# A swin block on one core: one multiplication of three tiles from VectorE to GpSimd, and one residual ahead of a transposition

## The reference

```python
attn = jax.nn.softmax(scores, axis=-1)
out = jnp.einsum('nhij,nhjd->nhid', attn, v)
out = out.transpose(0, 2, 1, 3).reshape(nw, L, c)
return out @ out_w.T + out_b
...
attn_out = attn_out @ proj_w.T + proj_b
...
y = shortcut + y
```

## Time and profile before

| | us |
|---|---|
| median of 3 runs | 88.78 |
| lowest, highest run | 88.52, 90.08 |
| profiled execution | 87.22 |
| its span, first to last instruction | 85.2 |

### The profile page before, as it was taken

The page is one execution under the profiler, slowest core; times in us unless marked ns, Lnnn a source line. Parts: engine busy times, 40 slices in busy tenths (PEclk is TensorE's granted clock), DMA queues, the critical chain, the costliest instruction groups (busy, mean ns, idle before and its releaser), DMA issues.

```text
span 85.2 us, 4265 instructions
## 1 busy us (share of the span) xinstructions
PE 79.6 (93%) x1786; PEld 48.0 (56%) x1786; DVE 64.7 (76%) x208; ACT 53.0 (62%) x89; POOL 46.8 (55%) x58
## 2 busy tenths in 40 slices
PE   5999999889999999799999999999999999999950
PEld 5987757555865767467566637465464423533420
DVE  4999998969789989989789999997943944333260
ACT  0396798879888476588288356664587664725400
POOL 7988829989862972997634675787204041300000
PEclk9999999999999999999999999999999999999998
DMA  0799600121101122101021120000000000032042
GB/s 19 203 331 439 258 31 8 36 66 33 53 32 53 51 84 78 53 1 38 32 100 56 52 64 6 8 0 8 0 8 0 0 0 0 13 118 86 38 162 84
DMA packets 3490, 5.75 MB, mean 67 GB/s; under 512 B 944, under 2 KB 1712, under 8 KB 3344
## 3 DMA queue, kind: packets, MB, share of 16 engines
q1 hardware_dynamic: 2608, 3.08, 10.9%
q10 hardware_dynamic: 864, 2.40, 7.3%
HBM read 2.66 MB, written 1.05 MB: 44 GB/s over the span
## 4 chain that ended last, share of the span: by engine, by line
PE 65%; DVE 18%; issue 8%; DMA 3%; ACT 2%; SPq 1%; DVEq 0%; ACTq 0%
PE ps_s L333 14%; PE ps_u L426 6%; PE ps_u L499 5%; DVE row_max L656 4%; PE ps_m L307 4%; PE ps_s L483 4%; PE ps_t L333 3%; PE ps_t L483 3%; DMA masked<-qk 3%; PE ps_o L467 3%; PE ps_m L483 2%; PE ps_t L409 2%; PE ps_m L297 2%; PE ps_o L499 2%; PE ps_o L442 2%
## 5 line engine op out<-in xcount | busy, mean ns | idle before, releaser
L1058 POOL TENSOR_TENSOR max_x<-max_t,early 128x512 bf16<-128x512 bf16 x14 | 14.7, 1048 | 10.6 <-DVE max_t L669 10.6
L656 DVE TENSOR_REDUCE row_max<-ps_s 128x16 f32<-128x1024 f32 x15 | 18.1, 1209 | 2.5 <-PE ps_s L333 2.2
L915 ACT ACTIVATE probs<-ps_t 128x1024 f32<-128x1024 f32 x13 | 13.3, 1023 | 8.8 <-PE ps_t L409 8.4
L333 PE MATMUL ps_s<-masked,qk 32*64 32x256 f32 x240 | 16.9, 387 | 1.0 <-ACT probs L915 0.4
L333 PE MATMUL ps_t<-masked,qk 32*64 32x256 f32 x224 | 15.5, 387 | 0.0
L1067 POOL TENSOR_TENSOR rstd<-y_var,minus_half 128x4 f32<-128x4 f32 x8 | 8.1, 1010 | 9.9 <-DVE y_var L719 9.8
L333 PEld LDWEIGHTS ps_s<-masked,qk 32*64 32x64 f32 x240 | 8.1, 131 | 5.9 <-issue 2.9
L426 PE MATMUL ps_u<-probs,vz 128*32 128x64 f32 x512 | 10.5, 222 | 0.0
L426 PEld LDWEIGHTS ps_u<-probs,vz 128*32 128x32 f32 x512 | 7.9, 109 | 3.1 <-issue 2.7
L1043 POOL TENSOR_TENSOR rstd<-var,minus_half 128x4 f32<-128x4 f32 x8 | 8.3, 1043 | 1.0 <-DVE var L644 0.4
L282 PE MATMUL ps_t<-zeros 128*128 128x128 f32 x32 | 6.9, 376 | 1.0 <-DVE zeros L817 1.0
(11 more groups left out here) (111 smaller groups left out, 150.6 us busy)
## 6 DMA issues: line engine op xcount, KB each, us to landing
masked<-qk SPq DMA_DIRECT2D x38, 32.0 KB, 2.0
x_ch<-x_ch_d ACTq DMA_DIRECT2D x1, 1024.0 KB, 8.0
out_d<-result SPq DMA_DIRECT2D x3, 256.0 KB, 2.5
x_tok<-x_tok_d ACTq DMA_DIRECT2D x1, 512.0 KB, 6.0
masked<-qk SPq DMA_DIRECT2D x8, 64.0 KB, 2.4
late<-late_d ACTq DMA_DIRECT2D x1, 352.0 KB, 5.2
x_tok<-x_tok_d SPq DMA_DIRECT2D x2, 128.0 KB, 3.4
x_tok<-x_tok_d ACTq DMA_DIRECT2D x1, 256.0 KB, 4.8
```

The lines of the kernel that those rows point to most:

```text
L333: return nc.tensor.matmul(ps[o:o + L, g, n * TOK:(n + 1) * TOK], qk[r:r + RG, b, w, t], masked[r:r + RG, b, :, w, t], start=(n == 0), stop ...
L656: nc.vector.tensor_reduce(row_max[:, w, 0:16], score_bank(k, w)[:].rearrange("q g (h j) -> q (g h) j", j=L), axis=AX.X, op=ALU.max).then_i ...
L915: nc.scalar.activation(probs[:, w, :], scores_t_bank(k, w)[:].rearrange("q g c -> q (g c)"), ACT.Exp).then_inc(probs_done, 1)
L1058: nc.gpsimd.tensor_tensor(max_x[:, k % 2, w, :].rearrange("q (n i) -> q n i", n=16), bf16_high(max_t[:, w, :]).unsqueeze(1).to_broadcast([ ...
```

## The change

On VectorE `scale_attn(k)` is left out for tiles 3, 4 and 5, and GpSimd does the same multiplication, right behind `spread_max(t+1, 0)` in slots 4, 5 and 6. It waits for the inverted sums of its tile and for `transpose_attn` of the tile before, which read the same buffer `attn_tok`. The semaphore `attn_scaled` is now raised by VectorE for five tiles and by GpSimd for three. Besides, in slot 2 VectorE's `residual(0)` stands ahead of `transpose_sums(1)` instead of behind `split_max(3, 0)`; the residuals of the other tiles stay where they were.

```diff
+        POOL_SCALED = (3, 4, 5)
...
+                if t == 2:
+                    residual(0)
                 if tile_ok(t - 1):
                     transpose_sums(t - 1)
                 if tile_ok(t + 1):
                     split_max(t + 1, 0)
-                if tile_ok(t - 2) and t - 2 not in SPLIT:
+                if t > 2 and t - 2 not in SPLIT:
                     residual(t - 2)
...
-                if tile_ok(t - 1):
+                if tile_ok(t - 1) and t - 1 not in POOL_SCALED:
                     scale_attn(t - 1)
...
+            def scale_attn(k):
+                pool.wait_ge(recip_done, k + 1)
+                pool.wait_ge(attn_done, k)
+                nc.gpsimd.tensor_tensor(attn_tok[:].rearrange("q n (u d) -> q n u d", u=2),
+                                        sums[:, :, 0:2 * D].rearrange("q n (u d) -> q n u d", u=2),
+                                        recip[:].unsqueeze(3).to_broadcast([P, 16, 2, D]),
+                                        op=ALU.mult).then_inc(attn_scaled, 1)
...
                 if tile_ok(t + 1):
                     spread_max(t + 1, 0)
+                if t - 1 in POOL_SCALED:
+                    scale_attn(t - 1)
```

## The result

| | kernel before | changed kernel |
|---|---|---|
| median of 8 runs | 88.87 | 89.17 |
| lowest, highest | 87.69, 90.16 | 88.96, 89.83 |
| span of the profiled execution | 85.2 | 87.7 |

The ratio of the changed kernel to the one before is 1.0233, 95% interval 1.0189 to 1.0278. It compares for each kernel the runs near its fastest, so it says more of the lower ends (88.96 against 87.69, which is 1.4%) than of the medians, which differ by 0.3%. Timed twice more, on two chips, the same changed kernel had ratios of 1.0100 (0.9995 to 1.0205) and 1.0117 (1.0051 to 1.0183); the kernel before, timed against itself, had 1.0066 (1.0015 to 1.0117) and 0.9990 (0.9921 to 1.0058). So by these timings the change costs about 1%, and the comparison itself can be off by more than half a per cent. I had forecast 0.4 us less.

The account below looks back on a forecast made before the run. TensorE, busy 93% of the span, was taken as the bound, with three holes of 0.77 us in all. Gains of 0.26 and 0.14 us summed to 0.40 us, for a forecast of 88.4 us, range 87.7 to 89.3.

Parts of the forecast that it names:

- the other 0.19 us of the hole: TensorE's 0.45 us hole at 34.46: the earlier exponential gains 0.26 us, then the shift of the scores holds the rest.
- part 1: Slot 2, VectorE: tile 0's residual ahead of the transposed sums lets ScalarE's exponential start at 33.48, not 33.74; gain 0.26 us.
- Part 1 brings nothing: Rival: something else holds the exponential in slot 2, leaving 0.14 us gained alone, 88.6 us; chance 0.10.
- Part 2's price: Slots 4 to 6: one GpSimd scaling of tiles 3 to 5 costs 0.61 us, range 0.42 to 1.05; gain 0.14 us.
- starts at about 46.86: Slot 4, VectorE: split_max starts then instead of 47.06, so transpose_attn could start 0.20 us earlier, at 47.21.
- the rival of the blocked split: Slots 4 and 5: split_max waits for GpSimd's scaling to end; loss 0.2 us, 88.7 us in all; chance 0.13.
- one pair of rows 0.02 us apart: split_max at 50.23 beside GpSimd's residual at 50.21 took 0.13 us, as with GpSimd idle; read as no blocking.
- Sum of the holes: TensorE's holes: 0.26 us from the moved residual plus 0.14 us from GpSimd's scalings, 0.40 us gained.
- the upper end of the range: 89.3 us, set between a GpSimd scaling of 1.05 us (88.8) and one of 1.5 us (89.7).
- No case but a scaling of 2 us is that large: Whole kernel: only GpSimd scalings of 2 us would reach the 2% (1.8 us) that can be told from no change.

Follow-up runs that it names:

- e3: Kernel before with only tile 0's residual moved ahead of the transposed sums in slot 2, GpSimd scaling nothing: 88.70 us, ratio 1.0032.
- e8: Kernel before with tile 0's residual moved ahead and, in slot 2, invert_sums(1) put behind find_max(3, 1): 88.39 us, ratio 1.0109.
- e4: Kernel before with only GpSimd scaling tiles 3 to 5, the residual not moved: 88.27 us, ratio 1.0057.
- e1: Kernel before, unchanged, run once more: 88.24 us, ratio 1.0066.
- e11: Kernel before, unchanged, run a third time for one more trace: 89.04 us, ratio 0.9990.
- e13: Kernel before with an added VectorE fill of 256 unused columns ahead of find_max(3, 1) in slot 2: 89.84 us, ratio 0.9950.
- e16: Second trace of the kernel before with tile 0's residual moved ahead and an added ScalarE copy of 256 unused columns ahead of exponentiate(2, 1): 90.08 us, single run.
- e5: Kernel before with 28 warm-up products of 32x16 in place of 7 of 128x128, 84 more TensorE instructions ahead of the work: 96.77 us, ratio 1.107.

## Why the prediction was wrong

- *"the other 0.19 us of the hole remain, because the shift is late next."* This is the step of part 1 that failed. What is late next is find_max(3, 1), which scores_ready waits for; it ended 0.06 us before the exponential in before, and the same edit put it 0.13 us later. The working on ScalarE was right to 0.01 us (33.48), and the 0.13 us on VectorE was right too (33.66 against 33.53). I used it only for find_max(4, 0), with 0.30 us of cover, and not for the maximum just ahead of that one, which had none. Gain 0.26 expected, none measured: the hole was 0.45 us before, and 0.47 in e3 and in all three executions of the changed kernel. e8, which moves that maximum forward too, has 0.26. "Part 1 brings nothing" had a chance of 0.10, and its reason was another holder of the exponential; it was another holder of the matmuls.
- *Part 2's price* was right: 0.63 us for 0.61. That split_max *"starts at about 46.86"* was right too (46.78 in e4); that transpose_attn then starts 0.20 us earlier failed, since the split beside a scaling ended only with the scaling. Gain 0.14 expected, a loss of some 0.05 measured in e4 (8.22 us for 8.17). That was the rival of the blocked split, with a chance of 0.13 and a loss of 0.2, which the rule of the Trainium skill (SBUF — State Buffer, Who interferes with whom) had named; every trace with the scaling agrees with it (splits of 0.32 to 0.70 us, ended 0.03 or 0.04 us after GpSimd's instruction; one that began 0.02 us before the scaling's end took the usual 0.17). I had set against it one pair of rows 0.02 us apart. Those pairs are too close to tell: in e4 a split that starts 0.04 us after GpSimd's residual takes 0.13 us (50.18 and 50.14), and one that starts 0.06 us after it takes 0.70 (55.48 and 55.42). A row that refutes a lock must lie well inside the other instruction.
- *Sum of the holes:* 0.40 us expected, nothing measured in either part. That the median, 89.17, lies inside the range of 87.7 to 89.3 is luck: the upper end of the range came from scalings of 1.05 to 1.5 us, and they took 0.63.
- *What was missing* is the term of the stops: 0.89 us a span in before, 2.42 changed. One of them stood in the timeline of before, at 41.5 us, and I passed over it, because a matmul was still recorded as running: five score matmuls took 0.91 us, where four just ahead of them took 0.39. "No case but a scaling of 2 us is that large" was wrong for that reason, by the first ratio (1.0233).

```profile
41.11 0.39 PE L333 MATMUL ps_s<-masked,qk 32*64 32x256 f32 x4
...
41.33 0.91 PE L333 MATMUL ps_s<-masked,qk 32*64 32x256 f32 x5
```

- *What stays open:* why the stops are more with the change, if they are, and what sets the moment at which a block is asked for. Each timing of the changed kernel has a ratio over 1, its three traces have the larger sums, and the mean of all its runs is 0.28, 0.72 and 0.86 us above that of the kernel before in the same timing (e1 and e11 counted in). This speaks against chance; no run shows a path from the two edits to the stops, and the one that I thought of fell (e13 to e16).

## What to carry to other kernels

When a wait is to be shortened, list every semaphore that the waiting instruction needs, with the time of each, for the profile names only the one that came last: a twin 0.06 us behind takes the whole gain. Before work is moved to GpSimd, look for two-operand VectorE instructions that will lie beside it. And where a trace has gaps with no releaser inside groups of equal instructions, number the queue: if the gaps lie 256 instructions apart, look at the DMA queue of the instructions: here TensorE waited for its own code there, and closing other holes gave nothing.

## What the runs showed of the hardware

TensorE's code comes in blocks of 256 instructions by DMA, and by the working of the table 0.4 to 3.7 us of a span of 85 to 88 us went into waiting for it in ten of its eleven executions (the eleventh had next to none); in the stretch from 22 to 60 us it executes a block in about 4 us.

The kernel with other warm-up products (e5) took 8 us more. Its granted clock reads 1.00 (2.4 GHz) in all stretches, yet between 10 and 20 us one score matmul took 0.642 us, as its groups by line show, against 0.387 in the kernel before. A group of 16 took 1.98 us at 13.59, and 1.09 at 29.18, which is what the same group takes in the kernel before, at 20.00. So by then e5 was 9.2 us late, and from there on it kept the pace of before but for stops. What had changed ahead of it is that TensorE had done 56 passes of 32x16 instead of 14 of 128x128. The last of these rows is of the kernel before.

```profile
L333 PE MATMUL ps_s<-masked,qk 32*64 32x256 f32 x16 | 2.0, 642 | 0.0
```

```profile
13.59 1.98 PE L333 MATMUL ps_s<-masked,qk 32*64 32x256 f32 x16
...
29.18 1.09 PE L333 MATMUL ps_s<-masked,qk 32*64 32x256 f32 x16
```

```profile
20.00 1.09 PE L333 MATMUL ps_s<-masked,qk 32*64 32x256 f32 x16
```
